# Five row terms a slot, two strided copies, and offset masks copied straight into PSUM

## The reference

```python
value = (xf @ vp_w.T + vp_b).reshape(n, L, G, cg)
om_in = depthwise_3x3(x) + dw_b
om    = om_in @ om_w.T + om_b            # per pixel and group: 9 x (dy, dx), 9 masks
py = h + base_y + off[..., 0];  px = w + base_x + off[..., 1]
y0, x0 = floor(py), floor(px);  ty, tx = py - y0, px - x0
sampled = (gather(y0, x0, (1-ty)*(1-tx)) + gather(y0, x0+1, (1-ty)*tx)
         + gather(y0+1, x0, ty*(1-tx))   + gather(y0+1, x0+1, ty*tx))
out = einsum('nhwgk,nhwgkc->nhwgc', mask, sampled) @ op_w.T
x = x + out
```

## Time and profile before

| | us |
|---|---|
| median of 3 runs (lowest, highest) | 2926.32 (2924.11, 2930.4) |
| profiled execution, its own time | 2924.83 |
| span of its instructions | 2923.0 |
| PE busy | 2430.8 (83%) |
| DVE busy | 2205.6 (75%) |
| ACT busy | 2259.7 (77%) |
| POOL busy | 1917.6 (66%) |

### The profile page before, as it was taken

One profiled execution on the slowest core, in us unless ns is written; L12 is line 12 of the kernel. 1 busy time (PEld: TensorE's weight loads), 2 busy tenths in 40 slices (PEclk: granted clock), 3 DMA queues, 4 the chain that ended last, 5 costly groups with the idle time before them and its releaser, 6 DMA issues. The chain is left out here.

```text
span 2923.0 us, 100581 instructions
## 1 busy us (share of the span) xinstructions
PE 2430.8 (83%) x40456; PEld 2021.2 (69%) x40456; DVE 2205.6 (75%) x3095; ACT 2259.7 (77%) x4721; POOL 1917.6 (66%) x1452
## 2 busy tenths in 40 slices
PE   3999779993688888888888888888888888888887
PEld 2666556772577777777777777777777777777786
DVE  3555423334989897989888898989898988989773
ACT  2444256662989889898989898898989898989892
POOL 1000000003888888888988888888988898988892
PEclk8999889996899999999999999999999999999998
DMA  4555579975577677777777777777778777877675
GB/s 103 130 132 144 143 182 265 263 199 172 124 191 203 181 195 192 188 191 190 204 194 192 187 200 195 197 183 193 199 189 198 188 196 187 206 179 190 177 176 147
DMA packets 356164, 538.18 MB, mean 184 GB/s; under 512 B 171728, under 2 KB 258256, under 8 KB 355536
## 3 DMA queue, kind: packets, MB, share of 16 engines
q1 hardware_dynamic: 296656, 422.71, 60.3%
q10 hardware_dynamic: 59136, 110.11, 10.8%
HBM read 312.82 MB, written 219.77 MB: 182 GB/s over the span
## 5 line engine op out<-in xcount | busy, mean ns | idle before, releaser
L1109 ACT ACTIVATE dwt<-xp,wts 128x224 f32<-128x224 f32 x2016 | 797.3, 484 | 40.8 <-ACT wst L1135 31.8
L1280 PE MATMUL acc_p<-abuf,vbd 128*32 128x136 f32 (+5 forms) x20480 | 710.4, 291 | 54.9 <-issue 46.0
L1280 PEld LDWEIGHTS acc_p<-abuf,vbd 128*32 128x32 f32 (+1 forms) x20480 | 645.9, 145 | 117.7 <-issue 60.5
L979 DVE TENSOR_TENSOR pr<-mh_p,ht 128x864 f32<-128x864 f32 x672 | 668.9, 1051 | 23.2
L1258 PE MATMUL win_p<-pr,smat 128*128 128x160 f32 x4032 | 626.7, 310 | 27.3 <-POOL pr L1065 15.8
L246 PE MATMUL cv<-cin,wb 128*64 128x392 bf16 x6912 | 590.4, 333 | 25.8 <-ACT cin L225 25.8
L1258 PEld LDWEIGHTS win_p<-pr,smat 128*128 128x128 f32 x4032 | 570.4, 194 | 51.2 <-issue 22.4
L246 PEld LDWEIGHTS cv<-cin,wb 128*64 128x64 bf16 x6912 | 401.4, 110 | 208.7 <-ACT cin L225 25.9
L1048 POOL TENSOR_TENSOR dwt<-dwt 128x896 f32<-128x896 f32 x224 | 516.3, 2305 | 4.7 <-ACT dwt L1109 4.7
L1062 POOL TENSOR_TENSOR pr<-pr 128x576 f32<-128x576 f32 x224 | 317.3, 1417 | 187.8 <-DVE pr L979 187.8
L1135 ACT ACTIVATE wst<-win_p 128x200 f32<-128x200 f32 x896 | 388.6, 605 | 62.4 <-PE win_p L1258 38.7
(11 more groups left out here) (132 smaller groups left out, 2674.9 us busy)
## 6 DMA issues: line engine op xcount, KB each, us to landing
abuf<-weight_scratch SPq DMA_DIRECT2D x1568, 96.0 KB, 3.3
weight_scratch<-wst ACTq DMA_DIRECT2D x112, 960.0 KB, 6.2
xt<-x SPq DMA_DIRECT2D x128, 392.0 KB, 7.6
rows_scratch<-vsb SPq DMA_DIRECT2D x224, 128.0 KB, 2.1
vbd<-rows_scratch SPq DMA_DIRECT2D x896, 32.0 KB, 3.2
x_scratch<-xt SPq DMA_DIRECT2D x64, 392.0 KB, 6.6
y<-x SPq DMA_DIRECT2D x64, 392.0 KB, 4.4
x3h<-x_scratch SPq DMA_DIRECT2D x64, 392.0 KB, 4.9
```

Of the source, the lines that this page charges most:

```text
L979: dve.tensor_tensor(pr[:, j % 2, slots, :, :, :].rearrange("p k e x z -> p e k (x z)"), mh[:, a, :, :].rearrange("p (k x) z -> p k (x z)", ...
L1109: ins = act.activation(dwt[:, j % 2, k, :].rearrange("p (r w) -> p r w", w=W), image[:, r:r + BR, k % 3:k % 3 + W], ACT.Identity, scale=dw ...
L1280: mm = pe.matmul(acc_p[32 * (2 * s + b):32 * (2 * s + b) + 32, 0:2 * TN].rearrange("p (t w r) -> p t w r", t=BR, r=2)[:, t0:t1 + 1, x0:x1, :],
```

## The change

The weights are kept for exactly five rows. A place of the weights shrinks from PC = 96 to 80 words, a band from 480 to 416, and the pieces that go through DRAM with them (96 to 82 KB in, 960 to 832 KB out). apply takes the rows that a row of the input reaches as runs: pairs where they are aligned, and a run of one row at either end where they are not. That makes 18 runs of 40 rows in all for a tile pair away from the edges, where there were 12 runs of 48 rows.

copy_weights becomes two copies of 400 elements, each of which writes rows k and k + 2 two words apart and reads every second word of win_p. For that the order inside a tile is now group before row (g k), and windows packs its five terms closely, so the fourth of them (e == 3) crosses a PSUM bank and is cut in two, columns 0 to 32 and 32 to 160.

On DVE copy_om is split: copy_offsets at the same place in the step, and copy_masks after products, which writes the masks of tile j+2 into the middle third of mh_p. mask_hats multiplies them from there, first into the outer thirds, then in place. om_ok, for which PE's next offset rows wait, is now given by copy_masks; the hats wait for off_ok.

```diff
-RP = RT + 1
-WP = 172
-PC = 2 * BR * RP * 2
-BAND = CT * PC
+RW = 4 * BR
+PC = RT * RW
+BAND = CT * PC + RW
...
-                def copy_om(i, j):
+                def offset_sums(i, j, to, lo, hi):
+                    return dve.tensor_tensor(
+                        to.rearrange("q w (g k) -> q (w g) k", k=BR),
+                        om_p[:, :].rearrange("q (k z) -> q z k", k=BR)[:, G * lo:G * hi, :],
+                        ombt[:, G * lo:G * hi].unsqueeze(2).broadcast_to([LANES, G * (hi - lo), BR]), ALU.add)
+
+                def copy_offsets(i, j):
                     dve.wait_ge(om_ready, NT * i + j + 1)
-                    dve.tensor_tensor(
-                        oms[:, j % 2, :, :].rearrange("q w (b k g) -> q (w b) k g", b=2, g=GS),
-                        om_p[:, :].rearrange("q (k z) -> q k z", k=BR)[:, :, 0:OMC].rearrange("q k (v g) -> q v k g", g=GS),
-                        ombt[:, :].rearrange("q (v g) -> q v g", g=GS).unsqueeze(2).broadcast_to([LANES, 6 * TAPS, BR, GS]),
-                        ALU.add).then_inc(om_ok, 1)
+                    offset_sums(i, j, oms[:, j % 2, :, :], 0, 2 * TAPS).then_inc(off_ok, 1)
+
+                def copy_masks(i, j):
+                    t = NT * i + j
+                    dve.wait_ge(om_ready, t + 1)
+                    wait(dve, pr_ok, 3 * t)
+                    offset_sums(i, j, mh[:, 1, :, :], 2 * TAPS, 3 * TAPS).then_inc(om_ok, 1)
 
                 def mask_hats(i, j):
-                    wait(dve, pr_ok, 3 * (NT * i + j))
-                    dve.wait_ge(hat_ok, NT * i + j + 1)
-                    dve.tensor_tensor(mh[:, :, :, :],
-                                      oms[:, j % 2, 2 * TAPS:3 * TAPS, :].unsqueeze(1).broadcast_to([LANES, 3, TAPS, BR * G]),
-                                      ht[:, j % 2, :, 0:TAPS, :], ALU.mult).then_inc(mh_ok, 1)
+                    t = NT * i + j
+                    dve.wait_ge(om_ok, t + 1)
+                    dve.wait_ge(hat_ok, t + 1)
+                    dve.tensor_tensor(mh[:, 0:3:2, :, :], mh[:, 1, :, :].unsqueeze(1).broadcast_to([LANES, 2, TAPS, BR * G]),
+                                      ht[:, j % 2, 0:3:2, 0:TAPS, :], ALU.mult).then_inc(outer_ok, 1)
+                    dve.wait_ge(outer_ok, t + 1)
+                    dve.tensor_tensor(mh[:, 1, :, :], mh[:, 1, :, :], ht[:, j % 2, 1, 0:TAPS, :], ALU.mult).then_inc(mh_ok, 1)
...
                     n = near(i, j, 2, first, last)
                     if n:
-                        copy_om(*n)
+                        copy_offsets(*n)
                     n = near(i, j, 1, first, last)
                     if n:
                         mask_hats(*n)
                         products(*n)
+                    n = near(i, j, 2, first, last)
+                    if n:
+                        copy_masks(*n)
...
-                    for k in range(BR):
-                        to = 2 * BR * (2 - 2 * (k % 2)) + BR * u + k
+                    for r in range(2):
+                        to = RW * (1 - r) + BR * u + r
                         cells = wst[:, 0, to:to + 1]
                         ins = act.activation(
-                            bass.AP(cells.tensor, cells.offset, [cells.ap[0], [PC, CT], [2 * BR, 2 * RT], [BAND, GS]]),
-                            win_p[:, 0:CT * WP].rearrange("p (e z) -> p e z", e=CT)[:, :, 0:RT * BR * G].rearrange(
-                                "p e (m k g) -> p e m k g", k=BR, g=GS)[:, :, :, k, :],
+                            bass.AP(cells.tensor, cells.offset, [cells.ap[0], [2 * BR, 2 * CT * RT], [BAND, GS], [2, 2]]),
+                            win_p[:, 0:CT * RT * BR * G].rearrange("p (m g k r) -> p r m g k", g=GS, k=2, r=2)[:, r],
                             ACT.Copy)
...
-                        to = WP * e
+                        cuts = (0, 1, RT) if e == 3 else (0, RT)
                         for n, (a, b) in enumerate(terms):
-                            mm = pe.matmul(win_p[:, to:to + 160], smat[:, e, :],
-                                           pr[:, j % 2, 0:RT, a, b, :],
-                                           start=n == 0, stop=n == len(terms) - 1)
+                            for m0, m1 in zip(cuts, cuts[1:]):
+                                mm = pe.matmul(win_p[:, BR * G * (RT * e + m0):BR * G * (RT * e + m1)], smat[:, e, :],
+                                               pr[:, j % 2, m0:m1, a, b, :],
+                                               start=n == 0, stop=n == len(terms) - 1)
...
-                        t0, t1 = max(0, yq - y0 - 2) // 2, min(2 * BR - 1, yq - y0 + 2) // 2
...
+                        k0, k1 = max(0, yq - y0 - 2), min(2 * BR - 1, yq - y0 + 2)
+                        t0, t1 = (k0 + 1) // 2, (k1 + 1) // 2
+                        runs = (((k0, 1, 1),) if k0 % 2 else ()) + (((2 * t0, t1 - t0, 2),) if t1 > t0 else ()) + (
+                            ((k1, 1, 1),) if k1 % 2 == 0 else ())
+                        for ka, n, r in runs:
```

More of the change, by code:

```diff
@@ L60 @@
 RT = 5
-RP = RT + 1
-WP = 172
-PC = 2 * BR * RP * 2
-BAND = CT * PC
+RW = 4 * BR
+PC = RT * RW
+BAND = CT * PC + RW
 PX = 4
-SEEN = (PX + CT - 1) * PC
+SEEN = (PX - 1) * PC + BAND
 LINE = GS * SEEN + PC
-QB = 36
-QC = 64
+QB = 37
+QC = 65
 VSLOT = 7
@@ L759, in l1_pass @@
         dwt = sb("dwt", [128, 2, TAPS, TN])
-        oms = sb("oms", [LANES, 2, 3 * TAPS, BR * G])
+        oms = sb("oms", [LANES, 2, 2 * TAPS, BR * G])
         ht = sb("ht", [LANES, 2, 3, 2 * TAPS, BR * G])
@@ L763, in l1_pass @@
         wst = sb("wst", [LANES, GS, BAND])
-        abuf = sb("abuf", [128, S, QC * PC])
+        abuf = sb("abuf", [128, S, QC * PC + RW])
         vsb = sb("vsb", [LANES, 2, GS, G, BR * 2])
@@ L789, in l1_pass @@
         tap_ok, dw1_ok, dw2_ok, dw3_ok, dw_ok = map(sem, ("tap_ok", "dw1_ok", "dw2_ok", "dw3_ok", "dw_ok"))
-        om_ready, om_ok, abs_ok, far_ok, hat_ok, mh_ok, pr_ok, mg1_ok, mg_ok = map(sem, (
-            "om_ready", "om_ok", "abs_ok", "far_ok", "hat_ok", "mh_ok", "pr_ok", "mg1_ok", "mg_ok"))
+        om_ready, off_ok, om_ok, outer_ok, abs_ok, far_ok, hat_ok, mh_ok, pr_ok, mg1_ok, mg_ok = map(sem, (
+            "om_ready", "off_ok", "om_ok", "outer_ok", "abs_ok", "far_ok", "hat_ok", "mh_ok", "pr_ok", "mg1_ok", "mg_ok"))
         win_ok, wst_ok, amat_ok, accs_ok, misc_ready, misc_ok, carried, passed = map(sem, (
@@ L1019, in _ @@
                     read_misc(j + 1, value=(0, j))
-                for j in range(2):
-                    copy_om(0, j)
+                copy_offsets(0, 0)
+                copy_masks(0, 0)
+                copy_offsets(0, 1)
                 mask_hats(0, 0)
                 products(0, 0)
+                copy_masks(0, 1)
                 for j in range(NT):
@@ L1115, in hats @@
                     t, u = NT * i + j, j % 2
-                    off = oms[:, u, 0:2 * TAPS, :]
+                    off = oms[:, u, :, :]
                     wait(act, pr_ok, 3 * (t - 1))
-                    act.wait_ge(om_ok, t + 1)
+                    act.wait_ge(off_ok, t + 1)
                     act.activation(ht[:, u, 1, :, :], off, ACT.Abs).then_inc(abs_ok, 1)
@@ new lines, in apply @@
+                        t0, t1 = (k0 + 1) // 2, (k1 + 1) // 2
+                        runs = (((k0, 1, 1),) if k0 % 2 else ()) + (((2 * t0, t1 - t0, 2),) if t1 > t0 else ()) + (
+                            ((k1, 1, 1),) if k1 % 2 == 0 else ())
+                        for ka, n, r in runs:
+                            opens = qb == 0 and yq == rows[0] and ka == k0
+                            for s in range(S):
+                                for b in range(2):
+                                    seen = abuf[0:K, s, :]
+                                    row = y0 + ka - yq + 3 - ka % 2
+                                    at = (QB * qb + x0 - 32 * qb + 2) * PC + RW * row + 2 * BR * b + ka
+                                    mov = bass.AP(seen.tensor, seen.offset + at, [seen.ap[0], [2 * RW + 2, n], [PC, x1 - x0], [1, r]])
+                                    mm = pe.matmul(
+                                        acc_p[32 * (2 * s + b):32 * (2 * s + b) + 32, 0:2 * TN].rearrange("p (t w r) -> p t w r", t=BR, r=2)[
+                                            :, ka // 2:ka // 2 + n, x0:x1, ka % 2:ka % 2 + r],
+                                        vbd[0:K, 1 - s, qb, yq // BR % VSLOT, :, :, 2 * (yq % BR) + b].rearrange("p g c -> p (g c)"),
+                                        mov, start=opens, stop=yq == rows[-1] and qb == 1 and ka == runs[-1][0],
+                                        skip_group_check=True)
```

## The result

The changed kernel takes 3100.8 us (median of 4 runs, 3097.55 to 3105.0), the kernel before 2925.2 beside it: ratio 1.060, interval 1.058 to 1.063. That is 176 us slower where 13 us faster was forecast, and above the range of 2878 to 2970. The profiled execution took 3105.0.

A forecast was written before the change was run, and what follows sets the result against it. No engine was full: waits between engines inside a step set the time. Step gains, nearly eaten by steps 4 and 8, summed to 134.8 against 135.62 us a pair, -13 us over 16 pairs: 2913 us, range 2878 to 2970.

The forecast's parts named there:

- the PE term: Apply and windows between PE's blocks: 6.3 us of PE work a step, just covered by DVE's 6.6.
- 0.1 to light steps for PE's own stalls: Allowance of 0.1 us in each step without a half sum, for PE's own stalls.
- PE becomes the bound: Rival: short apply records cost 23 ns (2933 us) or 28.8 ns (3120 us), so PE lengthens the steps; chance 0.14.
- the low bound: Apply's cheapest price, 0.215 ns a column and 6.4 ns a record: 144 records take 3.26 or 2.71 us a half.
- step 7 at 14.0: The pair's step with two half sums, 14.8 us before, was to take 14.0.
- the prices on DVE: The new offset and mask operations on DVE: 0.75 us for 576 elements, 0.45 for 288.
- the block moving behind DVE in light steps: In steps without a sum, PE's block no longer runs beside DVE but after the mask sums: 9.0 us a step.
- step 8 near 11.2: Step 8, with PE's clock lowered and a block of 4.50 us behind DVE, was to take 11.2 us.
- windows, +0.35 (3.06 for 22 against 2.71) for +0.33: PE's windows, going from 18 to 22 records, were to take 0.33 us more than 2.71.
- ACT's two copies: Two weight copies of 400 elements on ACT: 0.95 us for 1.74 before, counted as no gain in time.
- The lost turn of the sums: Rival: DVE's first sum starts behind POOL's next instruction, 2.2 us more in seven steps a pair, 3160 us; chance 0.08.
- the double price of PSUM: Rival: DVE's strided or in-place PSUM elements cost two each, at least 0.9 us a step, 3115 us; chance 0.10.

The follow-up runs named there:

- kernel 5: The changed kernel with windows issued after the first six rows of apply instead of behind all of it; 2959.1 us, 1.011 of the kernel before.
- kernel 1: The kernel before with only the DVE edit (copy_om split, masks copied behind the products, two mask products); 2962.2 us, 1.015 of the kernel before.
- kernel 13: As kernel 1, with all three loads of the next pair's fourth piece issued earlier, ahead of the weights' reads; 2944.6 us, 1.006 of the kernel before.
- kernel 6: As kernel 1, with copy_masks moved between the second and third product; 2893.7 us, 0.988 of the kernel before.
- 14: As kernel 6, with all three loads of the next pair's fourth piece issued earlier; 2874.2 us, 0.982 of the kernel before.
- 15: The changed kernel with windows inside apply, copy_masks between second and third product, and the three loads earlier; 2881.1 us, 0.981 of the kernel before.

## Why the prediction was wrong

**The step that failed** is the PE term: "PE needs 3.26 + 3.04 = 6.3 between blocks, DVE 0.15 + 0.81 + 5.64 = 6.6: covered, barely", with "0.1 to light steps for PE's own stalls". It counted columns and records and took the supply of instructions as free. apply's 96 products a half became 144, and the breaks went from 46.0 to 222.5 us, 0.99 a step over 224 steps instead of the 0.1, part of them followed by windows at a lower granted clock (3.59 us on average over the pass, 3.06 at full clock). Breaks of up to 1 us were covered, not only 0.3; longer ones went into the step: kernel 5, with 200 us less of them, is 142 us faster. The 46.0 us of "issue" inside apply stood in the trace of before, and the sum set against it 0.1 us in the light steps alone. The rival "PE becomes the bound" named the engine, at 28.8 ns a product; but where there is no break the products start nearly as fast as the low bound had it: 144 of 26 to 104 columns in 2.89 us, (2.89 - 0.225) / 143 = 18.6 ns apart, for a forecast of 2.71 in all. What binds is the supply of instructions, not the pitch of the products.

The Trainium skill (Runtime: NRT & Kernel Launch, "Instruction fetch mechanics") says that instructions come in blocks of 16 KiB, 256 to a block; 91 packets for 23,296 instructions agree. It also says that the fetch is hidden behind the pace of issue; the 222.5 us don't agree, and the measurement decides.

**The second step, mis-sized:** step 7 at 14.0. It took 15.7 in kernel 1 (1490.24 to 1505.96), because DVE comes to its sums before their loads, which SyncE issues behind eight reads of the weights (1492.47 to 1494.23), have landed; 14.1 once they are ahead. 1.7 us in 15 pairs are about 25 of the 49 us that kernel 1 loses against the forecast; where the rest goes, the scatter of 13 leaves open. In the changed kernel itself the wait hardly shows (6.9 us in all; step 7: 14.1), so it is no part of the 176 us worth naming; it comes back in kernel 5 (57.5 us), where the breaks are gone.

**Right:** the prices on DVE (0.77 and 0.47 us for 0.75 and 0.45), so PSUM at a stride of 1 KB or written over in place cost next to nothing here; the block moving behind DVE in light steps, 9.0; step 8 near 11.2 at a low clock (11.6 in the pair above, 10.6 on average over pairs 2 to 15); windows, +0.35 (3.06 for 22 against 2.71) for +0.33. ACT's two copies take 0.94 to 0.98 (forecast 0.95), and the time that they gain goes into waiting for the windows. The lost turn of the sums and the double price of PSUM did not happen.

## What to carry to other kernels

Before splitting a stretch of short products into more and shorter ones, look at the idle time that ends in "issue" in the middle of it: here each 128 products with their weight loads cost one packet of instructions, and the dense stretch outran them. Putting long products between two parts of such a stretch cost nothing here and gave back 142 us. A release that is moved to a later place joins engines into one loop: first move it as early inside that loop as its data allow (kernel 6 against 1: 69 us), and look which loads the shorter steps now overtake; kernels 14 and 15, with both, are 1.8 and 1.9% faster than the kernel before. The next bound then shows: in 15 apply stands 119.5 us for the weights' transfers.

## What the runs showed of the hardware that was not expected

PE stops up to 4.9 us in the middle of a list of products that wait for nothing, until a packet of 16,384 bytes has come over the instruction queue, which the page lists beside those of the data. Whether that packet is asked for too late, or stands behind data that fill the DMA engines (mostly nine tenths and more in the first cut of the break above), was not separated by a run. The trace of the changed kernel speaks for the data in the long breaks: in 24 the packet starts more than 0.3 us after PE has stopped, and in each of these the DMA engines are busy 84% or more from the stop to the packet's start (median over the pass: 62%). In the others the packet had started by then. In or after a long break the granted clock is lower: 0.76 in the stretch with the break of 3.96 us, 1.00 in the same step of kernel 13.
